# A cross-attention and two-expert-layer kernel: the mean square of a key's projection from one matmul over a folded, split sum

## The chip, the core and the metric

The kernel runs on one core of a Trainium2 chip. The metric is the device time of one execution in microseconds (us), lower is better. Three runs of the kernel before gave 1332.10, 1333.47 and 1333.48 us; the median is 1333.47.

## The reference, cut to what matters

The program is a chain of layers on 8 batches of 56 tokens of 256 numbers: a softmax cross-attention to 1500 context rows, a mixture-of-experts layer, a linear attention to the same context, and a second mixture. The change touches only the keys of the softmax attention. A key is a projection of a context row to 4 groups of 128 dimensions, and each group is divided by its root mean square:

```
def rms_norm(x, w, eps=EPS):
    xf = x.astype(jnp.float32)
    var = jnp.mean(xf * xf, axis=-1, keepdims=True)
    return w * (xf * jax.lax.rsqrt(var + eps)).astype(x.dtype)
```

Here the last axis has HEAD_DIM = 128 dimensions. Scores, softmax over 1500 keys and the weighted sum of the context follow. (The setup functions of the reference give weights; the whole is computed in float32.)

## The kernel before

Softmax attention is the function `softmax_attention`. It runs batch by batch (b = 0 to 7) and each batch in two units (u = 0 and 1), each with two of the four key groups. A unit has a part `scores` (the scores of 4 blocks of 112 rows against 3 pieces of 500 keys, exponentials behind it) and a part `unit`, a loop over 12 pieces t of 125 context rows: TensorE turns the probabilities (`turn`, tile ring), ScalarE and VectorE copy them as a high and a low part (pT), and six matmuls add the weighted context (csum).

float32 products are made of parts rounded to the fp32r type: a number is a high part (rounded) and a low part (the rest). `mm3` multiplies low by high, high by low and high by high.

Into the loop over t of each unit the keys of the next unit are woven, so that 15 of the 16 units carry 6 key steps each, 90 in all; the keys of the very first unit are made earlier. Key step i (0 to 5) has a part 0 and a part 1. The table SEQ sets the order on every engine: (0,0), (0,1), (1,0), (1,1), (0,2), (0,3), (1,2), (1,3), and so on: the first number is the part, the second i. So steps go in pairs (0,1), (2,3), (4,5). TensorE does entry t + 2 of the table behind the six csum matmuls of piece t (the first two ahead of the loop); ScalarE and VectorE do entry t at piece t; GpSimd walks through the table with nothing between.

What a key step does before the change, in order:

- TensorE: projection of 500 keys to 128 dimensions, 6 matmuls (proj).
- ScalarE: the square of 128x500 numbers into work (L1007).
- VectorE: the high part of the square, a copy to fp32r, sq[0] (L1092).
- GpSimd: the low part, work minus sq[0], into sq[1] (L1192).
- TensorE, part 1: two matmuls with a matrix of 1/128 (mean_mat), one for the low and one for the high part (L909). They average over the 128 partitions and put the mean on all of them. They wait for sq_lo, which GpSimd raises, and for ln_done of the step before, since the bank is one.
- ScalarE: logarithm and exponential (L1012, L1014), VectorE: product with proj and high part of the key (L1095, L1100), GpSimd: low part of the key (L1196).

Two other pieces of work lie on VectorE in the same loop. In a unit with u = 0 it makes the low part of the next batch's transposed context, six times (`split_t`, L1065, two inputs in SBUF), at t in SPLIT_AT. In a unit with u = 1 it rounds the next batch's context (`split_n`, L1072) and the next queries (L1080, L1083). GpSimd makes the 12 low parts of the context (L1206) behind the last key step of u = 1.

Every engine runs its own list in order and waits by semaphores. `work` and `sq` have two slots each, taken by i % 2.

Of the kernel before, what the change touches and what calls it, by code (L numbers as in the profile page):

```python
# [5 lines left out]
F32 = mybir.dt.float32  # L6
F32R = mybir.dt.float32r
ALU = mybir.AluOpType
ACT = mybir.ActivationFunctionType
# [13 lines left out]
KT = 12  # L23
# [786 lines left out]
def softmax_attention(nc, qT, rz, ctx_dram, ctxT_dram, wk, wv, raw_t, ct, kk, q, ident):  # L810
# [8 lines left out]
    with ExitStack() as ctx:  # L819
# [1 line left out]
        raw_n = p.sb("raw_n", [KP, 2, KT // 2, D])  # L821
        cn = [p.sb(f"cn{i}", [KP, KT, D], F32R) for i in range(2)]
        work = p.sb("work", [128, 2, CH])
        sq = [p.sb(f"sq{i}", [128, 2, CH], F32R) for i in range(2)]
        mean_mat = p.sb("mean_mat", [128, 128], F32R)
        pr = p.sb("pr", [TP, 4, SK])
        mn = p.sb("mn", [TP, 4, KC])
# [12 lines left out]
        t_loaded = [p.sem(f"t_loaded{c}") for c in range(KC)]  # L840
        n_loaded = [p.sem(f"n_loaded{i}") for i in range(2)]
        t_hi, t_lo, n_hi, n_lo, q_hi, q_lo = (p.sem(s) for s in ("t_hi", "t_lo", "n_hi", "n_lo", "q_hi", "q_lo"))
        proj_done, sq_done, sq_hi, sq_lo, mean_done, ln_done, rs_done = (p.sem(s) for s in (
            "proj_done", "sq_done", "sq_hi", "sq_lo", "mean_done", "ln_done", "rs_done"))
        k_full, k_hi, k_lo = (p.sem(s) for s in ("k_full", "k_hi", "k_lo"))
# [43 lines left out]
        def _(pe):  # L889
            def key_step(b, u, part, i):  # L890


                n = (2 * b + u - 1) * NS + i
                c, g = i // 2, 2 * u + i % 2
                if part == 0:
                    if u == 0 and i % 2 == 0:
                        wait(pe, t_lo, (b - 1) * PIECES + DC * (c + 1))
                    wait(pe, k_full, n - 1)
                    for d in range(DC):
                        last = mm3(nc, proj[:, i % 2, 0:CH], wk[0][:, d, g * HD:(g + 1) * HD],  # L900
                                   wk[1][:, d, g * HD:(g + 1) * HD], ct[0][:, c, d, :], ct[1][:, c, d, :], d == 0, d == DC - 1)
                    last.then_inc(proj_done, 1)
                else:
                    wait(pe, sq_lo, n + 1)
                    wait(pe, ln_done, n)
                    if i == 0:
                        wait(pe, out_free, 2 * b + u - 1)
                    for half in (1, 0):
                        last = nc.tensor.matmul(mean[:, 0:CH], mean_mat[:], sq[half][:, i % 2, :],  # L909
                                                start=(half == 1), stop=(half == 0))  # L910
                    last.then_inc(mean_done, 1)

            def output(b, u, ahead=NS):

# [79 lines left out]
        def _(act):  # L994
# [7 lines left out]
            def key_step(b, u, part, i):  # L1002
                n = (2 * b + u - 1) * NS + i
                if part == 0:
                    wait(act, proj_done, n + 1)
                    wait(act, k_lo, n - 1)
                    nc.scalar.activation(work[:, i % 2, :], proj[:, i % 2, 0:CH], ACT.Square,  # L1007
                                         bias=eps[:, 1:2]).then_inc(sq_done, 1)
                else:

                    wait(act, mean_done, n + 1)
# [48 lines left out]
        def _(dve):  # L1060
# [24 lines left out]
            def key_step(b, u, part, i):  # L1085
# [3 lines left out]
                if part == 0:  # L1089
                    wait(dve, sq_done, n + 1)  # L1090
                    wait(dve, mean_done, n - 1)
                    nc.vector.tensor_copy(sq[0][:, i % 2, :], work[:, i % 2, :]).then_inc(sq_hi, 1)  # L1092
                else:
                    wait(dve, rs_done, n + 1)
                    nc.vector.tensor_tensor(work[:, i % 2, :], proj[:, i % 2, 0:CH], work[:, i % 2, :],  # L1095
# [89 lines left out]
        def _(pool):  # L1185
            def key_step(b, u, part, i):

                n = (2 * b + u - 1) * NS + i
                c, gi = i // 2, i % 2
                if part == 0:  # L1190
                    wait(pool, sq_hi, n + 1)
                    nc.gpsimd.tensor_tensor(sq[1][:, i % 2, :], work[:, i % 2, :], sq[0][:, i % 2, :].bitcast(F32),  # L1192
                                            ALU.subtract).then_inc(sq_lo, 1)
                else:
                    wait(pool, k_hi, n + 1)
                    nc.gpsimd.tensor_tensor(kk[:, c, 2 + gi, :], work[:, i % 2, :], kk[:, c, gi, :].bitcast(F32),  # L1196
                                            ALU.subtract).then_inc(k_lo, 1)

# [682 lines left out]
```

## Time and profile before

| what | value |
| --- | --- |
| median of three runs | 1333.47 us |
| profiled execution: span from first to last instruction | 1333.7 us |
| TensorE matmul busy (PE) | 1208.5 us, 91% |
| VectorE busy (DVE) | 886.9 us, 67% |
| ScalarE busy (ACT) | 735.6 us, 55% |
| GpSimd busy (POOL) | 533.6 us, 40% |
| mean granted TensorE clock | 0.960 |

The profile gives no time of the profiled execution outside of its span, so the span stands for it; it is 0.2 us above the median. PE counts a matmul from its start to a modelled end, and matmuls overlap, so the distance between two starts tells more than the duration. PEld is the weight load, DVE is VectorE, ACT is ScalarE, POOL is GpSimd. A line such as L909 is a line of the kernel before. A bracket at the end of a row gives the idle time of that engine ahead of the instruction and whose end it was that ended the wait.

### The profile page before, as it was taken

To read this page: it belongs to the slowest core of one execution; us is meant where nothing else is said; L and a number is where in the kernel's file an instruction comes from. 1 tells how busy PE (TensorE), PEld (TensorE's weight loads), DVE (VectorE), ACT (ScalarE), POOL (GpSimd) and SP (SyncE) were. 2 spreads that over 40 slices of the span, in tenths; PEclk is the share of its full clock that TensorE was granted. 3 is DMA by queue.
4 is the path that set the end of the run, shared out by engine and by line. 5 is a ranking of instruction groups with operands and counts; after the bars stand their busy time and mean duration, and the time that the engine had idled before them with its cause. 6 is when DMAs were issued, how large, how long until landed. Compare 5 with 4: busy or idle time off the path is not lost. (4 is left out here: it accounts for less than half of the span.)

```text
span 1333.7 us, 27107 instructions
## 1 busy us (share of the span) xinstructions
PE 1208.5 (91%) x9559; PEld 1043.7 (78%) x9559; DVE 886.9 (67%) x1854; ACT 735.6 (55%) x1263; POOL 533.6 (40%) x554
## 2 busy tenths in 40 slices
PE   5999999999969999999999999999999587967897
PEld 4888888888748888888888888888888475844685
DVE  5656666566557788887888778888775665434543
ACT  4655565556536666566665666666665215412542
POOL 2432232323234463544635446354451334420451
PEclk9999999999979999999999999999999697978798
DMA  4111111110042011110111101100000510005000
GB/s 147 62 41 54 39 54 31 39 39 1 2 113 72 1 47 48 33 60 0 46 46 32 60 0 46 46 32 14 0 1 1 185 55 1 1 20 196 1 1 14
DMA packets 38746, 56.03 MB, mean 42 GB/s; under 512 B 3058, under 2 KB 37154, under 8 KB 38178
## 3 DMA queue, kind: packets, MB, share of 16 engines
q1 hardware_dynamic: 37874, 54.23, 12.8%
q10 hardware_dynamic: 816, 1.05, 0.2%
q8 instruction: 36, 0.59, 0.2%
q14 instruction: 20, 0.16, 0.0%
HBM read 54.81 MB, written 0.46 MB: 41 GB/s over the span
## 5 line engine op out<-in xcount | busy, mean ns | idle before, releaser
L1192 POOL TENSOR_TENSOR att_sq<-att_work,att_sq 128x500 fp32r<-128x500 f32 x90 | 120.4, 1338 | 159.7 <-DVE att_sq L1092 159.7
L1196 POOL TENSOR_TENSOR attention_kk<-att_work,attention_kk 128x500 fp32r<-128x500 f32 x90 | 122.1, 1357 | 153.0 <-DVE attention_kk L1100 153.0
L101 PE MATMUL att_csum<-att_pT,att_cn 125*128 125x448 f32 x384 | 156.5, 407 | 5.3 <-DVE att_pT L1141 4.6
L1018 ACT ACTIVATE att_pr<-att_pr,att_nmx 112x1500 f32<-112x1500 f32 (+1 forms) x96 | 108.5, 1130 | 72.1 <-DVE att_nmx L1129 72.1
L103 PE MATMUL att_csum<-att_pT,att_cn 125*128 125x448 f32 x384 | 141.1, 367 | 0.0
L102 PE MATMUL att_csum<-att_pT,att_cn 125*128 125x448 f32 x384 | 140.2, 365 | 0.0
L1141 DVE TENSOR_TENSOR att_pT<-att_ring,att_pT 125x448 fp32r<-125x448 f32 x192 | 118.2, 616 | 21.5 <-ACT att_pT L1034 21.3
L609 DVE SCALAR_TENSOR_TENSOR attention_kk<-kvs_keys_ps,kvs_bk,attention_kk 64x500 fp32r<-64x500 f32 x96 | 70.8, 738 | 92.0 <-ACT attention_kk L493 90.4
L1126 DVE TENSOR_SCALAR_CACHE_REDUCE att_pr<-att_ring 112x500 f32<-112x500 f32 x192 | 121.8, 675 | 6.2 <-PE att_ring L103 4.8
L364 PE MATMUL kvs_feat<-kvs_f,attention_kk 128*125 128x256 f32 x768 | 113.5, 285 | 10.3 <-DVE kvs_kp L681 10.1
L951 PEld LDWEIGHTS att_ring<-all_ident,att_pr 112*125 112x125 f32 x768 | 110.7, 190 | 14.4 <-ACT att_pr L1018 2.2
L1034 ACT ACTIVATE att_pT<-att_ring 125x448 fp32r<-125x448 f32 x192 | 102.5, 534 | 23.8 <-PE att_ring L951 23.8
L493 ACT ACTIVATE attention_kk<-kvs_keys_ps,kvs_bk 64x500 fp32r<-64x500 f32 x96 | 64.8, 675 | 92.0 <-PE kvs_keys_ps L103 90.7
L951 PE MATMUL att_ring<-all_ident,att_pr 112*125 112x112 f32 x768 | 111.3, 271 | 1.8 <-ACT att_pr L1018 1.8
L364 PEld LDWEIGHTS kvs_feat<-kvs_f,attention_kk 128*125 128x125 f32 x768 | 99.0, 187 | 15.5 <-issue 14.0
L1007 ACT ACTIVATE att_work<-att_proj,att_eps 128x500 f32<-128x500 f32 x90 | 60.8, 675 | 86.9 <-PE att_proj L103 86.9
L1095 DVE TENSOR_TENSOR att_work<-att_proj,att_work 128x500 f32<-128x500 f32 x90 | 60.9, 677 | 57.2 <-ACT att_work L1014 56.8
L101 PE MATMUL att_ring<-attention_kk,attention_q 128*112 128x500 f32 x192 | 77.6, 404 | 17.3 <-DVE att_pr L1126 12.0
L546 ACT ACTIVATE kvs_kp<-kvs_feat,kvs_zero 125x512 f32<-125x512 f32 x96 | 65.9, 686 | 43.5 <-PE kvs_feat L364 43.0
L1012 ACT ACTIVATE att_work<-att_mean,att_eps 128x500 f32<-128x500 f32 x90 | 61.1, 678 | 45.7 <-PE att_mean L909 45.7
L101 PEld LDWEIGHTS att_csum<-att_pT,att_cn 125*128 125x128 f32 x384 | 73.2, 191 | 15.3 <-DVE att_pT L1141 9.8
L1092 DVE CAST att_sq<-att_work 128x500 fp32r<-128x500 f32 x90 | 51.6, 573 | 39.8 <-ACT att_work L1007 39.8
(282 smaller groups left out, 3281.8 us busy)
## 6 DMA issues: line engine op xcount, KB each, us to landing
attention_raw_t<-in_ctxT SPq DMA_DIRECT2D x45, 500.0 KB, 4.1
att_raw_n<-in_ctx SPq DMA_DIRECT2D x16, 750.0 KB
w_gate<-in_gate SPq DMA_DIRECT2D x1, 2112.0 KB, 9.7
w_up<-in_up SPq DMA_DIRECT2D x1, 2112.0 KB, 14.3
kvs_raw_q<-in_wq SPq DMA_DIRECT2D x8, 256.0 KB, 4.0
wo_raw<-in_wo SPq DMA_DIRECT2D x4, 512.0 KB, 6.6
w_down<-in_down SPq DMA_DIRECT2D x1, 2048.0 KB, 18.4
w_gate<-in_gate SPq DMA_DIRECT2D x1, 1760.0 KB, 13.3
```

Source lines behind the costliest of these rows:

```text
L101: nc.tensor.matmul(out, w_lo, x_hi, start=start, stop=False, skip_group_check=True)
L102: nc.tensor.matmul(out, w_hi, x_lo, start=False, stop=False, skip_group_check=True)
L103: return nc.tensor.matmul(out, w_hi, x_hi, start=False, stop=stop, skip_group_check=True)
L364: last = nc.tensor.matmul(feat[0:KP, half, z], ks[:, c, 2 * half + g, y], f2[:, w, :], start=(w == 1), stop=(w == 0), skip_group_check=True)
L609: nc.vector.scalar_tensor_tensor(ks[64:128, c, 2 * m + h, :], keys_ps[y, 0:CH], bk[y, m:m + 1], ks[0:64, c, 2 * m + h, :].bitcast(F32), AL ...
L951: last = nc.tensor.transpose(ring[0:KP, t % 3, j * TP:(j + 1) * TP], pr[:, j, t * KP:(t + 1) * KP], ident[0:TP, 0:TP])
L1018: nc.scalar.activation(pr[:, j, keys], pr[:, j, keys], ACT.Exp, scale=-1.0, bias=nmx[:, j:j + 1], accum_out=z[:, 4 * u + j, c:c + 1]).then ...
L1034: nc.scalar.activation(pT[0][:, t % 3, :], ring[0:KP, t % 3, 0:QU], ACT.Copy).then_inc(pT_hi, 1)
L1126: nc.vector.tensor_scalar(pr[:, j, c * CH:(c + 1) * CH], ring[0:TP, c, 0:CH], -1.0, 3.0e38, ALU.mult, ALU.min, accum_out=mn[:, j, c:c + 1] ...
L1141: nc.vector.tensor_tensor(pT[1][:, t % 3, :], ring[0:KP, t % 3, 0:QU], pT[0][:, t % 3, :].bitcast(F32), ALU.subtract).then_inc(ring_free, 1)
L1192: nc.gpsimd.tensor_tensor(sq[1][:, i % 2, :], work[:, i % 2, :], sq[0][:, i % 2, :].bitcast(F32), ALU.subtract).then_inc(sq_lo, 1)
L1196: nc.gpsimd.tensor_tensor(kk[:, c, 2 + gi, :], work[:, i % 2, :], kk[:, c, gi, :].bitcast(F32), ALU.subtract).then_inc(k_lo, 1)
```

## The change

The 128 squares of a key are no longer split as they are. ScalarE writes the squares of dimensions 0 to 63 into work[0:64] and those of 64 to 127 into a new tile, high, on partitions 0 to 63: two activations of 64x500. VectorE adds the two and rounds the sum into sq[0:64]. GpSimd adds the same two once more into a new tile, folded, unrounded, and then subtracts the rounded sum from it; the low part goes to sq[64:128]. One matmul with mean_mat over the 128 partitions of sq adds high and low parts together. Some waits come with it, for the buffers.

```
-        sq = [p.sb(f"sq{i}", [128, 2, CH], F32R) for i in range(2)]
+        high = p.sb("high", [HD // 2, 2, CH])
+        folded = p.sb("folded", [HD // 2, CH])
+        sq = p.sb("sq", [128, 2, CH], F32R)
...
-                    for half in (1, 0):
-                        last = nc.tensor.matmul(mean[:, 0:CH], mean_mat[:], sq[half][:, i % 2, :],
-                                                start=(half == 1), stop=(half == 0))
-                    last.then_inc(mean_done, 1)
+                    nc.tensor.matmul(mean[:, 0:CH], mean_mat[:], sq[:, i % 2, :], start=True, stop=True)\
+                        .then_inc(mean_done, 1)
...
-                    nc.scalar.activation(work[:, i % 2, :], proj[:, i % 2, 0:CH], ACT.Square,
-                                         bias=eps[:, 1:2]).then_inc(sq_done, 1)
+                    wait(act, sq_lo, n - 1)
+                    nc.scalar.activation(work[0:HD // 2, i % 2, :], proj[0:HD // 2, i % 2, 0:CH], ACT.Square,
+                                         bias=eps[0:HD // 2, 1:2])
+                    nc.scalar.activation(high[:, i % 2, :], proj[HD // 2:HD, i % 2, 0:CH], ACT.Square,
+                                         bias=eps[0:HD // 2, 1:2]).then_inc(sq_done, 1)
...
-                    nc.vector.tensor_copy(sq[0][:, i % 2, :], work[:, i % 2, :]).then_inc(sq_hi, 1)
+                    nc.vector.tensor_tensor(sq[0:HD // 2, i % 2, :], work[0:HD // 2, i % 2, :], high[:, i % 2, :],
+                                            ALU.add).then_inc(sq_hi, 1)
...
+                    wait(pool, sq_done, n + 1)
+                    wait(pool, sq_lo, n)
+                    wait(pool, k_lo, n - i % 2)
+                    if i == 0 and u == 1:
+                        wait(pool, n_lo, (b + 1) * KT)
+                    nc.gpsimd.tensor_tensor(folded[:], work[0:HD // 2, i % 2, :], high[:, i % 2, :], ALU.add)\
+                        .then_inc(folds, 1)
                     wait(pool, sq_hi, n + 1)
-                    nc.gpsimd.tensor_tensor(sq[1][:, i % 2, :], work[:, i % 2, :], sq[0][:, i % 2, :].bitcast(F32),
+                    wait(pool, folds, n + 1)
+                    nc.gpsimd.tensor_tensor(sq[HD // 2:HD, i % 2, :], folded[:], sq[0:HD // 2, i % 2, :].bitcast(F32),
                                             ALU.subtract).then_inc(sq_lo, 1)
                 else:
                     wait(pool, k_hi, n + 1)
+                    wait(pool, sq_lo, n + 2 - i % 2)
```

The list of GpSimd at the start of the attention, before, from the low parts of the first context (att_cn) through the first pairs of key steps (L1192 is the low part of the squares, L1196 that of the key):

```order
L1206 TENSOR_TENSOR att_cn<-att_raw_n,att_cn 125x256 x12
L1192 TENSOR_TENSOR att_sq<-att_work,att_sq 128x500 x2
L1196 TENSOR_TENSOR attention_kk<-att_work,attention_kk 128x500 x2
L1192 TENSOR_TENSOR att_sq<-att_work,att_sq 128x500 x2
L1196 TENSOR_TENSOR attention_kk<-att_work,attention_kk 128x500 x2
```

The same place now:

```order
L1220 TENSOR_TENSOR att_cn<-att_raw_n,att_cn 125x256 x12
L1201 TENSOR_TENSOR att_folded<-att_work,att_high 64x500
L1205 TENSOR_TENSOR att_sq<-att_folded,att_sq 64x500
L1201 TENSOR_TENSOR att_folded<-att_work,att_high 64x500
L1205 TENSOR_TENSOR att_sq<-att_folded,att_sq 64x500
L1210 TENSOR_TENSOR attention_kk<-att_work,attention_kk 128x500 x2
L1201 TENSOR_TENSOR att_folded<-att_work,att_high 64x500
L1205 TENSOR_TENSOR att_sq<-att_folded,att_sq 64x500
```

A pair of key steps now has six instructions on GpSimd where it had four, and the two folds stand ahead of the two subtractions, each in front of its own.

On ScalarE, in a unit with u = 0, from the copy of a turned piece (att_pT) over the square of the second pair's first step to that of its second step, before:

```order
L1034 ACTIVATE att_pT<-att_ring 125x448
L1007 ACTIVATE att_work<-att_proj,att_eps 128x500
L1000 ACTIVATE attention_ct<-attention_raw_t 128x500
L1034 ACTIVATE att_pT<-att_ring 125x448
L1007 ACTIVATE att_work<-att_proj,att_eps 128x500
```

and now:

```order
L1038 ACTIVATE att_pT<-att_ring 125x448
L1009 ACTIVATE att_work<-att_proj,att_eps 64x500
L1011 ACTIVATE att_high<-att_proj,att_eps 64x500
L1001 ACTIVATE attention_ct<-attention_raw_t 128x500
L1038 ACTIVATE att_pT<-att_ring 125x448
L1009 ACTIVATE att_work<-att_proj,att_eps 64x500
L1011 ACTIVATE att_high<-att_proj,att_eps 64x500
```

Each square is two activations in the place of one; nothing else changes its place there.

## Rows read from the trace of the kernel before

**Rows 1.** Windows, softmax attention: length, busy PE, PEld, DVE, ACT, POOL, clock, DMA, GB/s

```profile
429.00:1012.00 583.00, 572.43 (x3024) 494.10 (x3023) 464.18 (x1016) 375.94 (x652) 285.07 (x252) 1.00 0.09 31
```

**Rows 2.** Instructions on tile att_sq: count, ns min/median/max, first and last start

```profile
L909 PE MATMUL att_mean<-att_sq,att_mean_mat x180: 386/390/620, 398.3 to 1006.2; 128*128 128x500 f32 x180
```

**Rows 3.** Groups by shape: GpSimd on 128 and 64 partitions, ScalarE on 64

```profile
L1586 POOL TENSOR_TENSOR moe_wd<-w_down,moe_wd 128x256 fp32r<-128x256 f32 x29 | 21.2, 730 | 0.0
L1586 POOL TENSOR_TENSOR moe_wd<-w_down,moe_wd 64x256 fp32r<-64x256 f32 x1 | 0.7, 725 | 0.0
L493 ACT ACTIVATE attention_kk<-kvs_keys_ps,kvs_bk 64x500 fp32r<-64x500 f32 x96 | 64.8, 675 | 92.0 <-PE kvs_keys_ps L103 90.7
```

**Rows 4.** Timeline, unit with u = 0, first pair: start us, us, instruction, [idle]

```profile
730.09 0.55 ACT L1034 ACTIVATE att_pT<-att_ring 125x448 fp32r<-125x448 f32 x1 [0.70 <-PE att_ring L951]
732.34 0.68 ACT L1007 ACTIVATE att_work<-att_proj,att_eps 128x500 f32<-128x500 f32 x1
733.55 1.26 POOL L1192 TENSOR_TENSOR att_sq<-att_work,att_sq 128x500 fp32r<-128x500 f32 x1 [2.27 <-DVE att_sq L1092]
735.37 0.62 PE L909 MATMUL att_mean<-att_sq,att_mean_mat 128*128 128x500 f32 x2
```

**Rows 5.** Timeline, same unit, second pair: ACT, DVE, POOL, PE

```profile
739.03 0.68 ACT L1007 ACTIVATE att_work<-att_proj,att_eps 128x500 f32<-128x500 f32 x1 [1.00 <-PE att_proj L103]
739.61 0.61 ACT L1000 ACTIVATE attention_ct<-attention_raw_t 128x500 fp32r<-128x500 f32 x1
742.05 0.68 ACT L1007 ACTIVATE att_work<-att_proj,att_eps 128x500 f32<-128x500 f32 x1 [1.39 <-PE att_proj L103]
...
740.30 0.67 DVE L1065 TENSOR_TENSOR attention_ct<-attention_raw_t,attention_ct 128x500 fp32r<-128x500 f32 x1
742.76 0.42 DVE L1092 CAST att_sq<-att_work 128x500 fp32r<-128x500 f32 x1 [1.26 <-ACT att_work L1007]
743.27 1.79 DVE L1065 TENSOR_TENSOR attention_ct<-attention_raw_t,attention_ct 128x500 fp32r<-128x500 f32 x1
...
738.84 1.26 POOL L1196 TENSOR_TENSOR attention_kk<-att_work,attention_kk 128x500 fp32r<-128x500 f32 x1 [0.61 <-DVE attention_kk L1100]
740.46 1.64 POOL L1192 TENSOR_TENSOR att_sq<-att_work,att_sq 128x500 fp32r<-128x500 f32 x1 [0.35 <-DVE att_sq L1092]
743.26 1.26 POOL L1192 TENSOR_TENSOR att_sq<-att_work,att_sq 128x500 fp32r<-128x500 f32 x1 [1.16 <-DVE att_sq L1092]
...
743.51 0.62 PE L909 MATMUL att_mean<-att_sq,att_mean_mat 128*128 128x500 f32 x2
745.62 0.62 PE L909 MATMUL att_mean<-att_sq,att_mean_mat 128*128 128x500 f32 x2
```

**Rows 6.** Timeline, unit with u = 1, second pair: ACT, POOL, PE

```profile
779.56 0.68 ACT L1007 ACTIVATE att_work<-att_proj,att_eps 128x500 f32<-128x500 f32 x1 [1.15 <-PE att_proj L103]
782.70 0.68 ACT L1007 ACTIVATE att_work<-att_proj,att_eps 128x500 f32<-128x500 f32 x1 [2.03 <-PE att_proj L103]
...
780.89 1.27 POOL L1196 TENSOR_TENSOR attention_kk<-att_work,attention_kk 128x500 fp32r<-128x500 f32 x1 [2.34 <-DVE attention_kk L1100]
782.52 1.27 POOL L1192 TENSOR_TENSOR att_sq<-att_work,att_sq 128x500 fp32r<-128x500 f32 x1 [0.35 <-DVE att_sq L1092]
784.14 1.26 POOL L1192 TENSOR_TENSOR att_sq<-att_work,att_sq 128x500 fp32r<-128x500 f32 x1 [0.35 <-DVE att_sq L1092]
...
784.16 0.62 PE L909 MATMUL att_mean<-att_sq,att_mean_mat 128*128 128x500 f32 x2
786.27 0.62 PE L909 MATMUL att_mean<-att_sq,att_mean_mat 128*128 128x500 f32 x2
```

**Rows 7.** Timeline, PE: two of its waits

```profile
636.88 0.48 PE L101 MATMUL att_ring<-attention_kk,attention_q 128*112 128x500 f32 x1 [1.40 <-DVE att_pr L1126]
1019.10 1.65 PE L951 MATMUL att_ring<-all_ident,att_pr 112*125 112x112 f32 x8 [1.81 <-ACT att_pr L1018]
```

**Rows 8.** Windows, around the second of these waits (columns as in rows 1)

```profile
1018.00:1024.00 6.00, 4.90 (x27) 4.88 (x28) 2.62 (x8) 3.50 (x9) 0.00 (x0) 0.72 0.01 3
```

More of the change, by code:

```diff
@@ L842, in softmax_attention @@
         t_hi, t_lo, n_hi, n_lo, q_hi, q_lo = (p.sem(s) for s in ("t_hi", "t_lo", "n_hi", "n_lo", "q_hi", "q_lo"))
+        folds = p.sem("folds")
         proj_done, sq_done, sq_hi, sq_lo, mean_done, ln_done, rs_done = (p.sem(s) for s in (
```

## The prediction, made before the changed kernel ran

> **What bounds the kernel now.** I read the windows first, stage by stage, then the instructions on the tile sq, then the timeline of single units. In the steady part of the softmax attention TensorE is busy 572.43 of 583.00 us at full clock [rows 1]; VectorE has 464, ScalarE 376 and GpSimd 285 us. So TensorE's list bounds this stage, and whatever it has to wait for is added to the time. The part that changes is its 180 matmuls on mean_mat [rows 2]. GpSimd half idle looks like room for more work, but what counts is the chain of one key step: square, high part, low part, mean. In the timeline I compared the end of the low part with the start of the mean's matmul. The reader is to see how little lies between: 0.56 us in the second step of a unit (733.55 + 1.26 = 734.81 against 735.37) [rows 4], 1.10 us in the fourth (744.52 against 745.62) [rows 5], 0.87 us in the fourth of a unit with u = 1 (785.40 against 786.27) [rows 6]. The least distance at which TensorE shows no wait is 0.37 us (782.52 + 1.27 = 783.79 against 784.16) [rows 6]; I estimate that the signal and the weight load need 0.3 us of it. The true slack is thus 0.26, 0.80 and 0.57 us. A key step's chain may grow by that much and no more.
>
> **What is removed.** One matmul in each of 90 key steps. Two of them take 0.62 us [rows 5] and one 0.39 us [rows 2], so they start 0.23 us apart: 90 x 0.23 = 20.7 us less on the engine that bounds.
>
> **What is added, on the chain.**
> ScalarE: two squares of 64x500. Half the partitions do not halve the time, 64x500 takes 675 ns [rows 3], as 128x500 does [rows 5]. The next activation starts 0.58 us after the first (739.61 against 739.03) [rows 5], so the squares end 1.26 us after their start instead of 0.68.
> VectorE: an add of two inputs in SBUF instead of a copy. The nearest row is the subtraction of `split_t`, 0.67 us against the copy's 0.42 us [rows 5].
> GpSimd: the fold, one instruction more. 64 partitions take 725 ns where 128 take 730 [rows 3], so fold and subtraction take 1.26 us each, as the subtraction before did [rows 5].
>
> **Fold and add want the same two tiles at the same moment.** The rows of `split_t`, a VectorE operation with two SBUF inputs, show what that costs. At 743.27, started 0.01 us behind a subtraction on GpSimd, it took 1.79 us in place of 0.67 and ended 0.54 us after GpSimd did (745.06 against 744.52). At 740.30, started 0.16 us ahead of GpSimd, it took its 0.67 us, and GpSimd's 1.26 became 1.64: it ended 1.13 us after VectorE [rows 5]. So either waits for the other, and add and fold together take 0.67 + 1.13 = 1.80 us in whichever order. The subtraction can only follow.
> The Trainium skill, "SBUF — State Buffer", section "SBUF: two separate sides", says it as a rule: VectorE and GpSimd share one pair of ports, held for a whole instruction, and the loser is blocked. Read strictly, add and fold would take 0.67 + 1.26 = 1.93 us; the row has 1.80. With some five such hand-overs in each later pair of a u = 0 unit, 14 pairs, the strict rule would make the sum below 14 x 5 x 0.13 = 9 us larger. I go by the rows.
>
> **The sum, pair by pair.** Fifteen units have key steps: 8 with u = 0 and 7 with u = 1, each with a first pair and two later ones.
>
> First pair. Its second square waits for ScalarE's own queue, not for TensorE, and the extra activation of the first square falls into ScalarE's idle 0.70 us [rows 4]. So the square still starts at 732.34 and ends at 733.60; add from 733.63, fold done 1.80 later at 735.43, subtraction until 736.74 with 0.05 for the signal; mean at 737.04 instead of 735.37, 1.67 later. One matmul fewer behind it: +1.44. 15 x 1.44 = 21.6 us.
>
> Later pair, u = 0, times from 739.03 [rows 5]. Squares end at 1.26. GpSimd is free at 1.07 (738.84 + 1.26). Add 1.29 to 1.96, fold until 3.09. Next on VectorE is `split_t`, already waiting, and it goes between fold and subtraction, ending 0.54 after the fold: until 3.63; subtraction until 4.8; mean at 5.1, where it was at 4.48. The second square comes at 3.02 as before (its projection lies ahead of the mean) and ends at 4.28; the add is blocked until 4.8 and ends at 5.34; fold until 6.47, `split_t` until 7.0, subtraction until 8.15; mean at 8.45, where it was at 6.59. Later by 1.86, less 0.23: +1.63. Seven batches have `split_t` for a following one: 14 x 1.63 = 22.8 us. The last batch has none: there the chain grows by 0.58 + 1.80 + 0.05 + 1.26 + 0.03 - 1.79 = 1.93, less slack 0.80 and matmul 0.23: 2 x 0.90 = 1.8 us.
>
> Later pair, u = 1, times from 779.56 [rows 6]. Here GpSimd is still at a key's low part from 1.33 to 2.60. If that stays so, the add is blocked until 2.60 and ends at 3.14, fold 4.27, then a short copy of `split_n` (0.2, an estimate) and the subtraction until 5.6; second add 6.15, fold 7.28, copy and subtraction 8.6; mean at 8.9 where it was at 6.71, less the matmul: +2.0. If the wait in the first pair lets VectorE work off its queue, so that the low part is done at 1.4, the same steps give add 2.0, subtraction 4.6, and in the second step (its square ends at 4.40) add 5.15, subtraction 7.75 and mean 8.05: +1.1. I take 1.3, nearer to the second, since TensorE's wait surely comes first. 14 x 1.3 = 18.2 us.
>
> Sum: 21.6 + 22.8 + 1.8 + 18.2 = 64.4 us. The waits behind it are 64.4 + 20.7 = 85 us. Behind a waiting mean stand TensorE's next turn and its six csum matmuls; ScalarE and VectorE have their pieces for these ready and wait for later ones, so nothing fills the gap. The profiled execution's 1333.7 us, which is 0.2 above the median, becomes 1398 us. The rest of the program is unchanged. The new waits of ScalarE and of GpSimd's key parts are for work that stands earlier in GpSimd's own list, at nothing. The 12 context parts behind u = 1 end later by the delay of a pair, as TensorE itself does.
>
> **Rivals.**
> A. Fold and add run side by side, because they are narrower than the rows of `split_t`: for it speaks that no row shows 64 partitions in such a case, against it both rows above. Then the chain is 0.08 + 1.26 + 0.05 + 1.26 = 2.65 us after the square instead of 1.79, with the activation +1.44. First pairs 1.44 - 0.26 - 0.23 = 0.95, later ones 0.41 (u = 0) and 0.64 (u = 1): 15 x 0.95 + 16 x 0.41 + 14 x 0.64 = 30 us, 1364 us.
> B. The chain is hidden after all: then only the matmuls count and the time is 1333.7 - 20.7 = 1313 us. For it speaks TensorE's load and GpSimd's idle half; against it a slack of 0.26 us in every first pair, where ScalarE's second activation alone is 0.58.
> C. The clock falls. A wait of 1.40 us left it at full speed in the steady part, one of 1.81 us was followed by a fall: around it the mean of 0.72 over 6 us means 3.4 us at the lower of the two levels, 1.2 GHz, so 1.7 us of work lost [rows 7, 8]. The waits that I expect, 1.3 to 1.7 us with a smaller one ahead in many pairs, lie between the two. If twenty of the 45 pairs drew such a fall, 20 x 1.7 = 34 us: 1432 us. "TensorE: Matmul & The Clock Gate" of the Trainium skill, section "HAM oscillation — how this bites in real kernels", tells of such repeated falls where waits come again and again between groups of matmuls; the row at 1.40 us without a fall speaks for less.
> That a fold which reads partitions 0 to 63 and a subtraction which writes 64 to 127 cost more on GpSimd can't be seen in the rows; it would add to the same side.
>
> **How the numbers follow.** Forecast 57%, 1398 us, its own range 1372 to 1420: the u = 1 pairs at 1.1 or 2.0 move it by -3 or +10, and `split_t` finding gaps in all later u = 0 pairs (0.90 in place of 1.63) by -10; twice that is allowed. A 17%, C 18%, B 5%, and 3% for a case in which gain and waits cancel. The range 1355 to 1435 takes in A and C and leaves out B and the worst of C. Under about 0.2% a measurement of this kernel can't tell a change from none: slower 0.92, same 0.03, faster 0.05.
>
> **What the profile will show.** If I am right: 90 matmuls on mean_mat, each second step of a pair behind a wait of 1.3 to 1.9 us for GpSimd's subtraction, some 85 us in all; adds on VectorE with durations of 0.67 us and of 1.2 us or more; the mean clock of the stage still 1.00. If A holds, the folds take 1.26 us beside adds of 0.67 and the waits come to some 50 us. If C holds, the windows of the stage show a clock under 1.00. I am wrong if TensorE shows no waits there.

## The result and the profile after

The changed kernel takes 1398.09 us (median of four runs, 1397.26 to 1400.51) against 1332.97 us for the kernel before beside it; the ratio over all these runs is 1.0493, 95% interval 1.0478 to 1.0507. It is 65 us slower, and the span of the profiled execution is 1396.9 us against 1333.7, 63.2 us longer. That execution took 1398.64 us as the metric counts it, 1.74 us more than its span: the span is not quite the time.

The first part of its page: busy us of each engine, share of the span, instructions.

```profile
PE 1208.9 (87%) x9469; PEld 1022.9 (73%) x9469; DVE 949.4 (68%) x1854; ACT 803.4 (58%) x1353; POOL 679.9 (49%) x644
```

TensorE has 90 instructions fewer and as many busy us: a matmul that starts behind a wait is recorded longer, and the matmul ahead of the wait no longer overlaps the next one. ScalarE has 68 us more, GpSimd 146, VectorE 62. The windows over the softmax attention's steady part, longer by 63 us than in [rows 1]:

```profile
429.00:1075.00 646.00, 576.46 (x2961) 477.67 (x2960) 528.32 (x1024) 441.84 (x740) 423.57 (x338) 1.00 0.09 29
```

TensorE is busy for 89% of this stage where it was for 98%, and the granted clock is still 1.00. The waits of the stage show what took its time (engine, line, whom it waited for: us in total, times, longest us):

```profile
PEld att_mean L911 <- POOL att_sq L1205: 84.5, 76, 1.9
PE att_mean L911 <- POOL att_sq L1205: 54.8, 61, 1.5
PE att_ring L101 <- DVE att_pr L1131: 12.2, 7, 1.7
```

The first line is new: the weight load ahead of the mean's matmul stands for GpSimd's low part, 84.5 us in all; the second is the matmul's own wait for the same. The third, for the scores' tiles, has the longest wait of TensorE's matmuls in the stage, 1.7 us; such a wait was 1.40 us before [rows 7]. And the instructions on the tiles of the chain (ns min/median/max), to be held against [rows 2, 5]:

```profile
L1096 DVE TENSOR_TENSOR att_sq<-att_work,att_high x90: 670/808/1750, 394.2 to 1066.1; 64x500 fp32r<-64x500 f32 x90
L1201 POOL TENSOR_TENSOR att_folded<-att_work,att_high x90: 1235/1524/2340, 396.1 to 1066.4; 64x500 f32<-64x500 f32 x90
L1205 POOL TENSOR_TENSOR att_sq<-att_folded,att_sq x90: 1233/1254/1500, 397.5 to 1068.1; 64x500 fp32r<-64x500 f32 x90
L911 PE MATMUL att_mean<-att_sq,att_mean_mat x90: 391/492/788, 399.0 to 1069.4; 128*128 128x500 f32 x90
```

The fold, alone 1.24 us, takes 1.52 in the median, and the add 0.81 where 0.67 is its least.

The timeline of the changed kernel (start us, us, instruction), the second step of a first pair in a unit with u = 0, to set beside [rows 4]:

```profile
582.61 0.67 ACT L1009 ACTIVATE att_work<-att_proj,att_eps 64x500 f32<-64x500 f32 x1
583.28 0.68 ACT L1011 ACTIVATE att_high<-att_proj,att_eps 64x500 f32<-64x500 f32 x1
...
583.99 0.67 DVE L1096 TENSOR_TENSOR att_sq<-att_work,att_high 64x500 fp32r<-64x500 f32 x1 [0.65 <-ACT att_high L1011]
...
584.04 1.75 POOL L1201 TENSOR_TENSOR att_folded<-att_work,att_high 64x500 f32<-64x500 f32 x1 [0.39 <-ACT att_high L1011]
585.94 1.24 POOL L1205 TENSOR_TENSOR att_sq<-att_folded,att_sq 64x500 fp32r<-64x500 f32 x1
...
587.23 0.50 PE L911 MATMUL att_mean<-att_sq,att_mean_mat 128*128 128x500 f32 x1 [1.35 <-POOL att_sq L1205]
```

The mean starts 4.62 us after the squares (587.23 - 582.61), where it was 3.03 (735.37 - 732.34) [rows 4]. The add starts 0.05 us ahead of the fold and runs unhindered; the fold ends 1.80 us after the add's start (585.79 - 583.99).

The same unit's second pair, to set beside [rows 5]:

```profile
590.80 0.67 ACT L1009 ACTIVATE att_work<-att_proj,att_eps 64x500 f32<-64x500 f32 x1 [1.19 <-PE att_proj L103]
593.84 0.67 ACT L1009 ACTIVATE att_work<-att_proj,att_eps 64x500 f32<-64x500 f32 x1 [0.59 <-PE att_proj L103]
...
592.20 0.67 DVE L1096 TENSOR_TENSOR att_sq<-att_work,att_high 64x500 fp32r<-64x500 f32 x1 [1.31 <-ACT att_high L1011]
592.80 0.67 DVE L1069 TENSOR_TENSOR attention_ct<-attention_raw_t,attention_ct 128x500 fp32r<-128x500 f32 x1
595.24 1.28 DVE L1096 TENSOR_TENSOR att_sq<-att_work,att_high 64x500 fp32r<-64x500 f32 x1 [1.24 <-ACT att_high L1011]
596.44 1.73 DVE L1069 TENSOR_TENSOR attention_ct<-attention_raw_t,attention_ct 128x500 fp32r<-128x500 f32 x1
...
592.25 2.34 POOL L1201 TENSOR_TENSOR att_folded<-att_work,att_high 64x500 f32<-64x500 f32 x1 [0.56 <-ACT att_high L1011]
594.73 1.25 POOL L1205 TENSOR_TENSOR att_sq<-att_folded,att_sq 64x500 fp32r<-64x500 f32 x1
596.12 1.52 POOL L1201 TENSOR_TENSOR att_folded<-att_work,att_high 64x500 f32<-64x500 f32 x1
597.77 1.50 POOL L1205 TENSOR_TENSOR att_sq<-att_folded,att_sq 64x500 fp32r<-64x500 f32 x1
...
596.04 0.50 PE L911 MATMUL att_mean<-att_sq,att_mean_mat 128*128 128x500 f32 x1 [0.56 <-POOL att_sq L1205]
599.33 0.50 PE L911 MATMUL att_mean<-att_sq,att_mean_mat 128*128 128x500 f32 x1 [1.12 <-POOL att_sq L1205]
```

The first fold takes 2.34 us, since the add and then `split_t` (L1069) run ahead of it, and the second `split_t` 1.73 us, behind the second fold. The means come 5.24 and 8.53 us after the pair's first square, where they came at 4.48 and 6.59 [rows 5].

Where TensorE's time went, as sums of the distances between the starts of its matmuls in the attention, by what comes before and after (worked out from the trace; before, after):

```
csum -> mean (about 0.2 each without a wait)       20.7    93.6
mean -> turn or csum (next start behind the mean)  22.3    31.2
mean -> mean (second matmul, and the output's)     42.9    22.4
ring -> ring (scores and turns)                   208.4   211.7
whole stage                                       672.8   737.1
```

So 72.9 us of waits for GpSimd's low part, 8.9 us behind them and 3.3 us among scores and turns stand against 20.5 us of matmuls no longer issued.

### The profile page after: what moved, and what is told of

The parts are those of the page before. It is cut to its first block and busy times, and to the rows that moved or that the text cites. A ratio compares the mean times of both kernels' runs of the same rounds, so it can differ in the third digit from the quotient of the medians.

```text
span 1396.9 us, 27396 instructions
## 1 busy us (share of the span) xinstructions
PE 1208.9 (87%) x9469; PEld 1022.9 (73%) x9469; DVE 949.4 (68%) x1854; ACT 803.4 (58%) x1353; POOL 679.9 (49%) x644
## 5 line engine op out<-in xcount | busy, mean ns | idle before, releaser
L1201 POOL TENSOR_TENSOR att_folded<-att_work,att_high 64x500 f32<-64x500 f32 x90 | 151.1, 1679 | 115.6 <-ACT att_high L1011 109.0
L1096 DVE TENSOR_TENSOR att_sq<-att_work,att_high 64x500 fp32r<-64x500 f32 x90 | 84.9, 943 | 71.3 <-ACT att_high L1011 70.2
L1146 DVE TENSOR_TENSOR att_pT<-att_ring,att_pT 125x448 fp32r<-125x448 f32 x192 | 117.5, 612 | 11.0 <-ACT att_pT L1038 10.9
L1205 POOL TENSOR_TENSOR att_sq<-att_folded,att_sq 64x500 fp32r<-64x500 f32 x90 | 116.3, 1292 | 15.7 <-DVE att_sq L1096 3.7
L952 PEld LDWEIGHTS att_ring<-all_ident,att_pr 112*125 112x125 f32 x768 | 111.0, 190 | 10.9 <-ACT att_pr L1022 2.2
L1009 ACT ACTIVATE att_work<-att_proj,att_eps 64x500 f32<-64x500 f32 x90 | 60.2, 669 | 62.2 <-PE att_proj L103 62.2
L911 PE MATMUL att_mean<-att_sq,att_mean_mat 128*128 128x500 f32 x90 | 44.0, 489 | 59.5 <-POOL att_sq L1205 58.7
L101 PE MATMUL att_ring<-attention_kk,attention_q 128*112 128x500 f32 x192 | 77.8, 405 | 20.0 <-DVE att_pr L1131 14.7
```

The source lines that it names most:

```text
L101: nc.tensor.matmul(out, w_lo, x_hi, start=start, stop=False, skip_group_check=True)
L952: last = nc.tensor.transpose(ring[0:KP, t % 3, j * TP:(j + 1) * TP], pr[:, j, t * KP:(t + 1) * KP], ident[0:TP, 0:TP])
L1146: nc.vector.tensor_tensor(pT[1][:, t % 3, :], ring[0:KP, t % 3, 0:QU], pT[0][:, t % 3, :].bitcast(F32), ALU.subtract).then_inc(ring_free, 1)
L1201: nc.gpsimd.tensor_tensor(folded[:], work[0:HD // 2, i % 2, :], high[:, i % 2, :], ALU.add)\
L1205: nc.gpsimd.tensor_tensor(sq[HD // 2:HD, i % 2, :], folded[:], sq[0:HD // 2, i % 2, :].bitcast(F32), ALU.subtract).then_inc(sq_lo, 1)
```

## The experiments

The ratio beside each time is against runs of the kernel before on the same chip. The experiments did not all run on one chip, and the kernel before took between 1332.5 and 1334.6 us beside them (medians), so differences of 2 or 3 us between two experiments say little by themselves. The theory throughout: the chain of a key step (squares, add with fold, subtraction) ends later than TensorE's other work covers, because it is made of more and longer operations and because add and fold shut each other out; TensorE pays each overrun.

**e1: the changed kernel without the fold.**

```
-                    nc.gpsimd.tensor_tensor(folded[:], work[0:HD // 2, i % 2, :], high[:, i % 2, :], ALU.add)\
-                        .then_inc(folds, 1)
...
-                    nc.gpsimd.tensor_tensor(sq[HD // 2:HD, i % 2, :], folded[:], ...
+                    nc.gpsimd.tensor_tensor(sq[HD // 2:HD, i % 2, :], high[:, i % 2, :], ...
```

> The changed kernel without GpSimd's fold: the subtraction reads the second half's squares in the place of the folded sum, so the low part leaves out the first half. Theory (the chain square, add with fold, subtraction sets the time): the chain shrinks from 4.6 to 5.5 us to 3.5 to 3.9 us, most waits of TensorE go; left are about 0.7 us in each first pair and 0.1 to 0.5 in later pairs, so about 1337 us (1325 to 1348). Rival 1 (the doubled squares on ScalarE are the cause): the time stays within 10 us of 1398. Rival 2 (the fold costs only its own 1.26 us in 45 odd steps, with no contention): 1398 - 57 = 1341 us too, told from the theory by the adds, which would be as long as before.

1339.52 us (ratio 1.0039, 1.0028 to 1.0051). The fold is worth 58.6 us of the 65, its own time on the chain and its collision with the add together. The adds fall to 672 ns in the median, which rival 2 excluded:

```profile
L1096 DVE TENSOR_TENSOR att_sq<-att_work,att_high x90: 670/672/1508, 396.3 to 1010.8; 64x500 fp32r<-64x500 f32 x90
PEld att_mean L911 <- POOL att_sq L1202: 28.6, 52, 1.0
```

**e2: one activation for the squares.**

```
-                    nc.scalar.activation(work[0:HD // 2, i % 2, :], proj[0:HD // 2, i % 2, 0:CH], ...
-                    nc.scalar.activation(high[:, i % 2, :], proj[HD // 2:HD, i % 2, 0:CH], ...
+                    nc.scalar.activation(work[:, i % 2, :], proj[:, i % 2, 0:CH], ACT.Square,
+                                         bias=eps[:, 1:2]).then_inc(sq_done, 1)
...
+            nc.vector.memset(high[:], 0.0).then_inc(eps_set, 1)
```

> The changed kernel with one activation of 128x500 for the squares; high is zero throughout, so the second half's squares are left out of the sum. Theory: each chain is 0.68 us shorter, of which first pairs give back about 0.6, u = 0 pairs 0.57, u = 1 pairs 0.7: 45 x 0.62 = 28 us, 1370 us (1362 to 1378). Rival 1 (ScalarE's second activation is the cause of all): 1313 to 1335 us. Rival 2 (it is hidden, the fold alone matters): 1398 us.

1377.33 us (1.0323, 1.0297 to 1.0349): 21 us less than the changed kernel, 7 less than forecast but inside its bounds. The second activation is a part of the loss, about a third of it, and neither the whole nor nothing.

**e3: the add reads one input from PSUM.**

```
-                    nc.vector.tensor_tensor(sq[0:HD // 2, i % 2, :], work[0:HD // 2, i % 2, :], high[:, i % 2, :],
+                    nc.vector.tensor_tensor(sq[0:HD // 2, i % 2, :], proj[0:HD // 2, i % 2, 0:CH], work[0:HD // 2, i % 2, :],
```

> The changed kernel with the add on VectorE taking one input from PSUM (the projection in the place of the second half's squares: these are left out of the rounded sum, the values are wrong there). Everything else as it is. Theory (add and fold collide because both read two inputs in SBUF): now they run side by side, add 0.67 us, fold 1.26 us, the chain is about 0.5 us shorter per odd step: 1375 us (1362 to 1382), and the fold no longer takes 1.5 to 1.9 us in first pairs. Rival (the time of the fold beside the add has another cause, such as 64 partitions or GpSimd's own pace): time and the fold's duration stay, 1398 us and 1.74 us in first pairs.

1370.64 us (1.0272, 1.0244 to 1.0300): the same number of instructions of the same lengths, 27 us less. Add and fold of this kernel:

```profile
L1096 DVE TENSOR_TENSOR att_sq<-att_proj,att_work x90: 658/671/673, 395.0 to 1039.2; 64x500 fp32r<-64x500 f32 x90
L1201 POOL TENSOR_TENSOR att_folded<-att_work,att_high x90: 1238/1258/1410, 396.5 to 1039.3; 64x500 f32<-64x500 f32 x90
```

No add is longer than 673 ns (1750 in the changed kernel), and the fold is 1258 ns in the median in place of 1524. So the two collide while both read two inputs in SBUF, and no longer when the add takes one of them from PSUM. That both are narrow does not keep them apart, and neither of the two is slow by itself. The collision is worth 27 of the 65 us; the rest of the fold's 58.6 us in e1 would be its own length, 1.26 us against the add's 0.67, for which the subtraction waits even when nothing blocks it; no run shows that part alone. Rival A, for which the prediction gave 1364 us, is what this kernel shows, and the changed kernel did not.

**e4: a second matmul again.**

```
-                    nc.tensor.matmul(mean[:, 0:CH], mean_mat[:], sq[:, i % 2, :], start=True, stop=True)\
+                    for half in (1, 0):
+                        last = nc.tensor.matmul(mean[:, 0:CH], mean_mat[:], sq[:, i % 2, :],
+                                                start=(half == 1), stop=(half == 0))
```

> The changed kernel with a second, equal matmul on mean_mat in each key step (the mean is counted twice). Theory: in the first step of a pair the second matmul only takes from the wait of the second step, in the second step it counts: 45 x 0.23 = 10 us, 1408 us (1405 to 1412). Rival (TensorE's work counts in full, as a waiting list would if the waits did not depend on one another): 90 x 0.23 = 20.7 us, 1419 us.

1406.92 us (1.0553, 1.0517 to 1.0590): 9 us more, not 20.7. By the distances of starts the waits ahead of the mean fell by 12 us, from 73 to 61: a matmul that only fills a wait is free. So of the 20.7 us that the change saved, more than half went straight into longer waits.

**e5: VectorE makes the unrounded sum.**

```
-                    nc.vector.tensor_tensor(sq[0:HD // 2, i % 2, :], work[0:HD // 2, i % 2, :], high[:, i % 2, :],
-                                            ALU.add).then_inc(sq_hi, 1)
+                    nc.vector.tensor_tensor(high[:, i % 2, :], work[0:HD // 2, i % 2, :], high[:, i % 2, :],
+                                            ALU.add).then_inc(folds, 1)
+                    wait(dve, folds, n + 1)
+                    nc.vector.tensor_copy(sq[0:HD // 2, i % 2, :], high[:, i % 2, :]).then_inc(sq_hi, 1)
...
-                    nc.gpsimd.tensor_tensor(folded[:], work[0:HD // 2, i % 2, :], high[:, i % 2, :], ALU.add)\
```

> VectorE makes the unrounded sum (in place, in high) and then the rounded copy; GpSimd only subtracts. The whole result is computed. Theory: chain 1.36 (squares) + 0.7 (add) + 0.45 (copy) + 0.1 + 1.26 = 3.9 us, 4.3 beside a split of the context, against 4.6 to 5.5 us: waits left 1.1 us in first pairs, 1.0 in u = 0 pairs, 0.6 in u = 1 pairs, with 0.12 us each for the weight load behind a wait: 1312 + 45 = 1357 us (1345 to 1368). Rival (VectorE becomes the bound, since it gets 90 x 0.42 us more): slower than 1398 us.

1354.55 us (1.0164, 1.0146 to 1.0182). An instruction more on VectorE in the place of one on GpSimd gives 43.5 us back, though VectorE is the busier: the chain counts, not the load.

**e6: the mean of each second step a piece later.** On TensorE alone the table's entries (1,1), (1,3) and (1,5) stand behind the next piece's csum:

```
+        LATER = {0: [(1, 0)], 2: [(1, 1), (0, 2)], 3: [(0, 3)], 4: [(1, 2)], 6: [(1, 3), (0, 4)], 7: [(0, 5)],
+                 8: [(1, 4)], 10: [(1, 5)]}
...
-                    if keys and t + 2 < len(SEQ):
-                        key_step(*keys, *SEQ[t + 2])
+                    if keys:
+                        for entry in LATER.get(t, ()):
+                            key_step(*keys, *entry)
```

> The changed kernel with TensorE's mean of each second step one piece later (behind the next turn and csum, ahead of the next projection). The whole result is computed. Theory: the second step's wait of 1.0 to 1.5 us is covered by 1.6 us of other matmuls; the waits of the first steps stay (0.2, 0.3 to 0.7 us): 1312 + 24 + 5 = 1341 us (1332 to 1355). Rival (the delay only moves on: the projection two entries later waits for the key to be normalised): 1370 to 1400 us.

1400.51 us (1.0517, 1.0487 to 1.0546): nothing gained, the theory's 1341 us missed by 60. Its waits:

```profile
PEld att_mean L913 <- POOL att_sq L1208: 41.8, 38, 1.6
PEld att_ring L101 <- DVE att_pr L1134: 32.5, 32, 3.1
```

Half of the wait for the low part went. The waits of the second steps are gone, as forecast, but those of the third and fifth step, the first of the next pair, grew (the table under e10 has both). Moreover the key's logarithm, product and rounding stand in ScalarE's and VectorE's lists between pieces pT and ahead of the scores' first piece, and these came later in turn: by the distances of starts, scores and turns cost 14.7 us more than in the changed kernel, the way to csum 11.9 and csum itself 10.9. TensorE shows no wait at the projection's buffer, named as the rival's place; the delay did move on, to VectorE's list. A part of these sums is the clock: the scores' wait, up to 1.75 us in the changed kernel, is 2.63 or 2.64 us in seven units, and around the end of three of these waits the clock fell to the lower of its levels, 1.2 GHz, for 3.4 us. By the distances of starts the three falls cost 4.1 us.

**e7: e5 and e6 together.** The core of both edits:

```
-                    nc.vector.tensor_tensor(sq[0:HD // 2, i % 2, :], work[0:HD // 2, i % 2, :], high[:, i % 2, :],
+                    nc.vector.tensor_tensor(high[:, i % 2, :], work[0:HD // 2, i % 2, :], high[:, i % 2, :],
...
-                        key_step(*keys, *SEQ[t + 2])
+                        for entry in LATER.get(t, ()):
+                            key_step(*keys, *entry)
```

> Both: the sum on VectorE and the mean of each second step one piece later. The whole result is computed. Theory: chain 3.9 to 4.3 us against room of 4.48 us in first steps and 4.4 to 5.0 in second ones, no waits left: 1312 us and a few, 1313 to 1322 us, less than the kernel before. Rival (waits appear elsewhere, at the projection's buffer or in VectorE's queue): 1330 us or more.

1368.35 us (1.0266, 1.0248 to 1.0284), 14 us more than e5 alone. The wait for the low part is down to 23.3 us, and the scores wait for VectorE:

```profile
PEld att_ring L101 <- DVE att_pr L1135: 29.5, 28, 2.8
PEld att_mean L912 <- POOL att_sq L1206: 23.3, 28, 1.1
```

Behind the scores' waits the clock fell. The windows of e5 and of e7 over the same stretch (columns as in [rows 1]) and one of e7's waits with matmuls behind it:

```profile
429.00:1060.00 631.00, 588.78 (x3090) 498.16 (x3089) 516.17 (x1145) 451.17 (x760) 285.70 (x253) 1.00 0.09 30
429.00:1060.00 631.00, 588.89 (x3010) 493.87 (x3009) 530.18 (x1138) 444.48 (x752) 286.06 (x253) 0.98 0.09 30
...
738.71 0.48 PE L101 MATMUL att_ring<-attention_kk,attention_q 128*112 128x500 f32 x1 [2.39 <-DVE att_pr L1135]
...
740.62 0.62 PE L102 MATMUL att_ring<-attention_kk,attention_q 128*112 128x500 f32 x1
741.04 0.62 PE L103 MATMUL att_ring<-attention_kk,attention_q 128*112 128x500 f32 x1
...
744.67 0.39 PE L102 MATMUL att_ring<-attention_kk,attention_q 128*112 128x500 f32 x1
744.90 0.39 PE L103 MATMUL att_ring<-attention_kk,attention_q 128*112 128x500 f32 x1
```

Seven units have a wait of 2.38 to 2.41 us ahead of their scores, where e5 has 1.70 to 1.72, and behind six of them the clock fell to 1.2 GHz for 3.4 us: matmuls that start 0.23 us apart at full clock (744.67, 744.90) start 0.42 us apart there (740.62, 741.04). By the distances of starts the six falls cost 9.0 us, most of the 14 that e7 lost against e5. So the prediction's rival C, which the changed kernel did not show, is at work here. Without these falls e7 would still not beat e5: what the means no longer wait, 19.3 us, is taken up by longer waits for VectorE ahead of the scores and of csum.

**e8: VectorE makes all parts of the squares, GpSimd the context's low parts.**

```
+                    wait(dve, sq_hi, n + 1)
+                    nc.vector.tensor_tensor(sq[HD // 2:HD, i % 2, :], high[:, i % 2, :], sq[0:HD // 2, i % 2, :].bitcast(F32),
+                                            ALU.subtract).then_inc(sq_lo, 1)
...
-                nc.vector.tensor_tensor(ct[1][x], raw_t[x], ct[0][x].bitcast(F32), ALU.subtract).then_inc(t_lo, 1)
+                nc.gpsimd.tensor_tensor(ct[1][x], raw_t[x], ct[0][x].bitcast(F32), ALU.subtract).then_inc(t_lo, 1)
```

> VectorE makes the sum of the squares, its rounded copy and its low part; GpSimd makes no squares' parts any more and takes the low parts of the next batch's context (split_t) from VectorE. The whole result is computed. Theory: chain 1.36 + 0.7 + 0.45 + 0.7 = 3.2 us, against room of 2.8 us in the second step of a first pair (0.4 wait and 0.12 for the weight load, 15 times) and 3.3 to 4.5 us elsewhere: 1312 + 8 us, and up to 12 for blocked copies on VectorE: 1320 to 1333 us, 1326 in the middle, less than the kernel before. Rival (VectorE, with 60 us more of squares' low parts and 43 less of context, is late for the pieces pT): 1340 us or more.

1372.47 us (1.0289, 1.0272 to 1.0306): the rival. The wait for the squares falls to 28.5 us, but VectorE is busy 572 of 631 us of the stage and late for its pieces:

```profile
PE att_csum L101 <- DVE att_pT L1144: 20.8, 49, 0.8
PE att_mean L910 <- DVE att_sq L1094: 16.9, 26, 1.2
```

**e9: e8 with the first pairs' second mean a piece later.** The edit of e6 with a table in which (1,1) alone is moved:

```
+        LATER = {0: [(1, 0)], 2: [(1, 1), (0, 2)], 3: [(0, 3)], 4: [(1, 2)], 5: [(1, 3)], 6: [(0, 4)], 7: [(0, 5)],
+                 8: [(1, 4)], 9: [(1, 5)]}
...
-                        key_step(*keys, *SEQ[t + 2])
+                        for entry in LATER.get(t, ()):
+                            key_step(*keys, *entry)
```

> The same, and in first pairs alone TensorE's mean of the second step one piece later. Theory: the 8 us of waits in first pairs go: 1313 to 1326 us, 1319 in the middle. Rival (the key's normalising comes later by a piece and VectorE's queue with it, as in e6 and e7): no better than e8.

1375.16 us (1.0310, 1.0291 to 1.0330): no better than e8, as the rival says.

**e10: e5 with the same table.**

```
-                    nc.vector.tensor_tensor(sq[0:HD // 2, i % 2, :], work[0:HD // 2, i % 2, :], high[:, i % 2, :],
+                    nc.vector.tensor_tensor(high[:, i % 2, :], work[0:HD // 2, i % 2, :], high[:, i % 2, :],
...
+        LATER = {0: [(1, 0)], 2: [(1, 1), (0, 2)], 3: [(0, 3)], 4: [(1, 2)], 5: [(1, 3)], 6: [(0, 4)], 7: [(0, 5)],
+                 8: [(1, 4)], 9: [(1, 5)]}
```

> e5 with TensorE's mean of the second step one piece later in first pairs alone. Later pairs, the last one above all, keep their place, so VectorE is not behind at the start of the scores as in e7. Theory: of 15 waits of 1.1 us most go, 1354.5 - 15 = 1340 us (1336 to 1348). Rival (the delay moves on whatever the pair): 1352 us or more.

1351.81 us (1.0138, 1.0119 to 1.0158), 3 us less than e5 in place of 15, at the rival's bound; the intervals of the two ratios overlap. The waits ahead of the mean by step of a unit, worked out from the distances of starts (less 0.20 us each, summed over the 15 units), tell where the gain went:

```
step of the unit      1st   2nd   3rd   4th   5th   6th   (us)
kernel before         0.2   0.0   0.1   0.0   0.0   0.1
changed kernel        2.0  20.3   7.0  17.4   9.2  17.4
e5                    0.2  15.5   0.1  11.1   1.9  10.1
e10                   0.2   0.0   9.7   8.3   2.8  10.1
e7                    0.2   0.0   9.6   0.0   9.5   0.0
e6                    1.8   0.2  18.5   0.1  18.3   0.0
```

The first pair's second step waited 15.5 us in e5 and not at all in e10; but the third step, the first of the next pair, waited 0.1 and now 9.7 us. In ScalarE's list the squares of the next pair stand behind the logarithm and the exponential of the delayed step, so they come later with it. e7, which delays the second step of each pair, shows it at both later pairs, with 9.6 and 9.5 us, and e6 with 18.5 and 18.3.

**e11: the kernel before with one matmul.**

```
-                    for half in (1, 0):
-                        last = nc.tensor.matmul(mean[:, 0:CH], mean_mat[:], sq[half][:, i % 2, :],
-                                                start=(half == 1), stop=(half == 0))
+                    last = nc.tensor.matmul(mean[:, 0:CH], mean_mat[:], sq[0][:, i % 2, :], start=True, stop=True)
```

> The kernel before with one matmul on mean_mat in each key step; the squares' low part is still made and waited for, but left out of the mean. Theory: the chain is unchanged and its slack of 0.5 us or more covers the 0.23 us by which TensorE is earlier, so all of it counts: 1333.5 - 20.7 = 1313 us (1311 to 1317). Rival (other waits take most of the gain, since VectorE and ScalarE pace TensorE too): 1325 us or more.

1318.21 us (0.9876, 0.9853 to 0.9900), 16.4 us less and not 20.7. The distances of starts give 21.1 us less between the mean's matmuls, and 7.4 us more on the way to csum and within it: TensorE runs into VectorE's pT (9.8 us of waits where it had 4.7). That is the whole worth of the saved matmul, with its chain left alone; since the low part is missing from the mean, this kernel is a measure and not a version to use.

**e12: the kernel before with two activations for the square.**

```
+                    for half in range(2):
+                        y = slice(half * (HD // 2), (half + 1) * (HD // 2))
+                        last = nc.scalar.activation(work[y, i % 2, :], proj[y, i % 2, 0:CH], ACT.Square, bias=eps[y, 1:2])
+                    last.then_inc(sq_done, 1)
```

> The kernel before with the square of a key made by two activations of 64 partitions in the place of one of 128. The whole result is computed. Theory: the chain grows by 0.68 us; the slack in first pairs is 0.5, so there 0.2 wait and 0.12 for the weight load, 15 times, and nothing elsewhere: 1333.5 + 5 = 1338 us (1335 to 1343). Rival (ScalarE's time counts in full): 90 x 0.68 = 61 us, 1395 us.

1344.25 us (1.0063, 1.0041 to 1.0085), 9.7 us more by the medians. That is a little over the bound, by less than the interval is wide, and far from the 61 us of the rival. The wait for the low part is 7.4 us in 14 first pairs:

```profile
PEld att_mean L909 <- POOL att_sq L1194: 7.4, 14, 0.6
```

## Why the prediction was right

The forecast was 1398 us and the median is 1398.09; the mechanism and its terms hold, but a match that close is luck. Terms were off in both directions, and the forecast set the span equal to the time: the span grew by 63.2 us where 64.4 was forecast, and the 1.74 us between span and time of the profiled execution made up for it.

- Bound and slack. TensorE bounds, and the true slack in a first pair is half a us: e12 used it up with 0.68 us on ScalarE and paid 10 us. The change was bound to cost by its chain. The 0.3 us kept for signal and weight load were in truth 0.05 from subtraction to mean (587.18 to 587.23), so that the first pair's slack was 0.5 and not 0.26. Another 0.10 is paid behind the wait: the matmul is 0.50 us long instead of 0.39, and the next start is later by 0.10 in most cases.
- The matmul: 20.7 us forecast, 20.5 us measured in the changed kernel, but worth 16.4 when it is removed alone (e11), and 9 where chains set the waits (e4). The sum subtracted it once for each pair, 10 us, which is what e4 shows.
- The squares end 1.36 us after their start, not 1.26: the second activation starts 0.69 us after the first, not 0.58. The 0.58 was read behind a square of 128x500 and not behind one of 64x500. The signal from fold to subtraction takes 0.15 us, not 0.05. These two add 0.2 us to each chain, and the smaller 0.05 behind it takes 0.25 off.
- Add and fold: 1.80 us forecast, 1.80 us measured in the first pair. e3 shows that the collision is what makes it so.
- First pair: mean later by 1.67 us forecast, 1.59 measured. Later pair, u = 0: means at 5.1 and 8.45 forecast, 5.24 and 8.53 measured; the pair grew by 1.84 us (12.10, from 590.80 to the next pair's square at 602.91, against 10.26) where 1.63 was said. There `split_t` went ahead of the fold and not between fold and subtraction; the sum is the same. Later pair, u = 1: +1.0 where 1.3 was taken between 1.1 and 2.0; the low part of the key was out of the way, as the prediction held likely. Two units grew by 8.6 us (92.0 against 83.4) where 8.7 was forecast.
- Waits. The sum's 85 us came out as 81.8 us at the mean (72.9 and 8.9) and 3.3 us among scores and turns. A second step waits 1.2 to 1.4 us on the mean over the units, at the lower end of the forecast 1.3 to 1.9 or under it; the first steps of later pairs wait 0.5 to 0.6 us.
- Rivals. A needed add and fold side by side; e3 made them so and came to 1370.64 us, against 1364. B, the hidden chain, is refuted by the waits. C did not come: the clock of the stage stays 1.00, through waits of up to 1.75 us on TensorE. The 1.81 us wait behind the stage [rows 7, 8] was followed by a fall here too, but by none in e5 and e10. At 2.38 us and more, in e6 and e7, nine of fourteen waits were followed by one, so the rival was a sound one, though not for this kernel's waits.
- The rule of the Trainium skill in "SBUF — State Buffer", section "SBUF: two separate sides", agrees in substance, e3 above all: with one input from PSUM the block is gone. Its strict sum, 1.93 us, is 0.13 over the 1.80 measured, so the two overlap by that much at the change from one to the other.

Not tried: a version that makes the unrounded sum without VectorE and GpSimd. None of the versions that compute the whole result beats the kernel before; of those with the folded sum e10, at 1.0138, comes nearest. In e10 the waits ahead of the mean fell by 7.8 us in all (38.9 to 31.1 by the table), of which the time shows 2.7. Most of the rest went to the way from the turn to csum, which grew by 4.5 us (14.0 to 18.5 by the distances of starts): csum waits there for VectorE's pT, 3.6 us in seven waits of up to 0.6.

## What to carry to other kernels

That an engine is busy 98% of a stage does not mean that a matmul saved on it is time saved: look first at how much room the chain behind it has in each step, here half a us, and add up what the change puts on that chain. Two engines that get the same two inputs at the same signal are not two engines if their operations exclude each other; one input from PSUM, or the sum made once and handed on, is worth more than the balance of their loads. Moving a late consumer back in its own list only helps if those that follow it on other engines have room in their lists too. And a wait of the bounding engine can cost more than its length: look at the granted clock behind the longest waits, as in e7.

## What was unexpected of the hardware

- Two activations of 64x500 start 0.69 us apart (median of 90, the same in e12), where an activation behind the one square of 128x500 started 0.58 us after it [rows 5]. The memory that they read does not explain it: in the kernel before, the copy of a turned piece, read from PSUM, came 0.58 us behind the 128x500 square as well, and in e12 the copy of the context, read from SBUF, came 0.70 us behind a 64x500 one. The cause stays open.
- Where a mean had to wait for its signal, its weight load is recorded to start with the matmul (both at 587.23) and not 0.20 us ahead of it (735.17 against 735.37 before), and the next matmul starts 0.10 us later than it would: 8.9 us over the stage.
- While a two-input operation of VectorE and one of GpSimd overlapped, either order was seen: `split_t` ran ahead of a waiting fold in one step of a pair and behind it in the next (592.80 and 596.44).
- Waits of TensorE of up to 1.75 us left its clock at full speed throughout the changed kernel's stage, 1.81 us did so in e5 and e10 but not in the kernel before, and 2.38 to 2.64 us did so in five of fourteen cases (e6, e7).
